# Band transfers of the attention head stage: described in four-byte words, and their reads issued by ScalarE

## The chip, the cores and the metric

The kernel runs on one core of a Trainium2 chip. The metric is device time in microseconds (us), the median of several runs. Beside the runs there is one profiled execution, from which all rows below come. Engines are named as in the profile: PE (TensorE matmul), PEld (its weight loads), DVE (VectorE), ACT (ScalarE), POOL (GpSimd), SP (SyncE, which issues transfers). SPq and POOLq are the sequencers of SP and POOL.

## What is computed

Four residual sublayers work on 2048 tokens of width 256: self-attention with 16 heads of width 16, a mixture of experts, a gated delta-rule attention, and a quantized feed-forward layer. Only the first one touches the change:

```python
q = (x @ q_w.T + q_b).reshape(B, S, H, Dh).transpose(0, 2, 1, 3)
k = (x @ k_w.T + k_b).reshape(B, S, H, Dh).transpose(0, 2, 1, 3)
v = (x @ v_w.T + v_b).reshape(B, S, H, Dh).transpose(0, 2, 1, 3)
q = apply_rope(q)
k = apply_rope(k)
attn = jnp.einsum('bhqd,bhkd->bhqk', q, k) * scaling
probs = jax.nn.softmax(attn, axis=-1)
```

## The kernel before

The program runs phase after phase. The first is `head_phase`, which makes Q, K and V; the second is `attention_phase`. A phase ends when every engine has done its instructions in it, and the next begins after that.

**What `head_phase` makes.** Q and K are kept as three bf16 parts each (high, middle, low), so that bf16 matmuls give float32 scores. For the score matmul each head needs a column of 96 rows, six bands of 16, in the tensors `q_t` and `k_t`. The projections come out with heads across the partitions, so the parts go through a scratch tensor in HBM, `qk_dram`, to change their layout: written by blocks, read back by bands.

**Blocks.** There are 16 blocks, n = 0 to 15. A block is one half of the heads (u), one of Q and K (side) and 512 tokens (b). Four blocks in a row (a group) share u and side; the groups come as Q, K, K, Q, for the halves 0, 0, 1, 1. Three buffers `parts` take the blocks in turn (`DEEP` = 3). The steps of one block are:

- PE projects it (L314); DVE adds the bias and applies the rotary tables (L389, twice); POOL adds the two products to `whole` (L277).
- `highest(n)` on ACT (L350) copies `whole` to bf16, the first part. It first waits until block n - 3 has been written out of the same buffer.
- DVE subtracts it (L396). `middle(n)` on ACT (L354) copies the rest to bf16. ACT's order is highest(n), middle(n - 1), highest(n + 1), and so on.
- `lowest(n)` on POOL (L282) makes the third part.
- `parts_away(n)` on SP (L235) writes the three parts to `qk_dram`, one transfer each: 128 partitions with a run of 512 bf16 (1 KB) each, 128 KB in all.

**Bands.** `heads_back(m)` on SP (L243) waits until the four blocks of group m have been written, and then reads the group back in three transfers, of 48, 32 and 16 rows. A row is 8 heads of 2048 tokens in bf16, 32 KB in one run, and goes to one partition. The three are 1536, 1024 and 512 KB, 3 MB a group. Below, R0 to R3 are the reads of groups 0 to 3, each of three transfers.

**Order on SP before.** All transfers of this stage are issued by SP, in program order: blocks 0 to 4, R0, blocks 5 to 8, R1, blocks 9 to 12, R2, blocks 13 to 15, R3.

**What waits for what.** `attention_phase` waits for R0 and R1 before its first matmul (heads of the first half), and for R2 and R3 only when it comes to the second half, in the middle of the phase. DVE's last work in `head_phase` are eight additions that take V out of PSUM (L414); they stand behind DVE's work on block 15 in its order.

Of the kernel before, what the change touches and what calls it, by code (L numbers as in the profile page):

```python
# [12 lines left out]
F32 = mybir.dt.float32  # L13
BF16 = mybir.dt.bfloat16
# [8 lines left out]
T = 2048  # L23
# [5 lines left out]
HEADS, DH = 16, 16  # L29
# [18 lines left out]
def flat(ap):  # L48
    names = "abcde"[: len(ap.shape) - 1]
    return ap.rearrange(f"p {' '.join(names)} -> p ({' '.join(names)})")  # L50
# [122 lines left out]
def head_phase(c, a, QT, KT, V, heads_in):  # L173

    nc = c.nc
    GROUPS, TILES = 4, NT // 4
    BT = TILES * P
    BLOCKS_QK = 4 * GROUPS
    HALF = HEADS // 2
    DEEP = 3  # L180
    PART_AT = ((0, 1, 2), (2, 1, 0))
    with ExitStack() as ctx:  # L182
# [11 lines left out]
        cosp, sinp, whole, rest = ([work[:, 2 * m + i, :] for i in range(2)] for m in range(4))  # L194
        parts = [f(f"parts{i}", [P, 3, BT], BF16) for i in range(DEEP)]
        tp = [c.ps(ctx, f"hd_tp{i}", [P, 2, KD, P]) for i in range(2)]
        plain = [c.ps(ctx, f"hd_plain{i}", [P, BT]) for i in range(2)]
        turned_ps = [c.ps(ctx, f"hd_rotated{i}", [P, BT]) for i in range(2)]
        v_ps = [c.ps(ctx, f"hd_v_ps{i}", [P, 2, D]) for i in range(2)]
# [3 lines left out]
        stats_done, var_done, rstd_done, scaled, _, turned, copied, _ = c.norm.values()  # L203
# [6 lines left out]
        parts_out = [c.sem(ctx, f"hd_parts_out{i}") for i in range(DEEP)]  # L210
        block = ctx.enter_context(nc.Block())

        def place(n):
            return n // (2 * GROUPS), (0, 1, 1, 0)[n // GROUPS], n % GROUPS

        @block.sync
        def _(sp):
            x = a["x"].rearrange("(t p) d -> p t d", p=P)
            for g in range(GROUPS):
                sp.dma_start(c.X[:, TILES * g:TILES * g + TILES, :], x[:, TILES * g:TILES * g + TILES, :]  # L220
                             ).then_inc(x_in[g], 16)
            sp.dma_start(W, a["wqkv"]).then_inc(s["w_in"], 16)
            sp.dma_start(bias[:, :], a["bqk"]).then_inc(s["tables_in"], 16)
            sp.dma_start(v_bias[:, :, :], a["bv"]).then_inc(s["tables_in"], 16)
            sp.dma_start(tables, a["rope"]).then_inc(s["tables_in"], 16)
            sp.wait_ge(s["one_set"], 1)
            sp.dma_start(KT[SPLIT_ROWS:SCORE_ROWS, 1:HEADS, :],
                         KT[SPLIT_ROWS:SCORE_ROWS, 0:1, :].broadcast_to([MAX_ROWS, HEADS - 1, T])
                         ).then_inc(s["ones_in"], 16)

            def parts_away(n):
                u, side, b = place(n)
                sp.wait_ge(s["lo_done"], n + 1)
                for part in range(3):
                    sp.dma_start(a["qk_dram"][side, u, part, :, :, BT * b:BT * b + BT].rearrange("d h t -> h d t"),  # L235
                                 parts[n % DEEP][:, part, :]).then_inc(parts_out[n % DEEP], 16)

            def heads_back(m):
                u, side, _ = place(GROUPS * m)
                for n in range(GROUPS * m, GROUPS * m + GROUPS):  # L240
                    sp.wait_ge(parts_out[n % DEEP], 48 * (n // DEEP + 1))
                for band, first, n in ((0, 0, 3), (3, side, 2), (5, 2 * side, 1)):
                    sp.dma_start(flat((QT, KT)[side][DH * band:DH * (band + n), HALF * u:HALF * u + HALF, :]),  # L243
                                 a["qk_dram"][side, u, first:first + n, :, :, :].rearrange("c d h t -> (c d) (h t)")
                                 ).then_inc(heads_in[u], 16)

            for n in range(BLOCKS_QK):
                parts_away(n)
                if n % GROUPS == 0 and n:
                    heads_back(n // GROUPS - 1)  # L250
            heads_back(BLOCKS_QK // GROUPS - 1)
            sp.wait_ge(s["ones_in"], 16)

        @block.gpsimd
        def _(pool):
# [17 lines left out]
            def put_together(n):  # L273
                pool.wait_ge(s["rot_read"], n + 1)
                if n >= 2:
                    pool.wait_ge(s["rest_done"], n - 1)
                pool.tensor_tensor(whole[n % 2], cosp[n % 2], sinp[n % 2], ALU.add  # L277
                                   ).then_inc(s["whole_done"], 1)
# [5 lines left out]

            for n in range(BLOCKS_QK + 1):
                if n < BLOCKS_QK:
                    put_together(n)
# [4 lines left out]
        def _(pe):  # L292
# [11 lines left out]
            def project(n):  # L304
                u, side, b = place(n)
                cols = 2 * P * (2 * u + side)
                if n < GROUPS:
                    pe.wait_ge(copied, was["copied"] + 2 * n + 2)
                for out, at, read, done in ((plain, cols, s["plain_read"], s["plain_done"]),
                                            (turned_ps, cols + P, s["rot_read"], s["rot_done"])):  # L310
                    if n >= 2:
                        pe.wait_ge(read, n - 1)
                    for k in range(KD):
                        last = pe.matmul(out[n % 2][:, :], W[:, k, at:at + P], c.XT[:, k, BT * b:BT * b + BT],  # L314
                                         start=(k == 0), stop=(k == KD - 1))
                    last.then_inc(done, 1)
# [11 lines left out]
            for g in range(GROUPS):  # L328
# [3 lines left out]
                else:  # L332
                    project(g - 1)
            for n in range(GROUPS - 1, BLOCKS_QK):
                project(n)
# [3 lines left out]
        @block.scalar  # L339
        def _(act):  # L340
            for i in range(NT // 2):
                act.wait_ge(turned, was["turned"] + i + 1)
                act.activation(c.XT[:, :, 2 * i * P:(2 * i + 2) * P].rearrange("p k (j c) -> p j k c", j=2),
                               tp[i % 2][:, :, :, :], ACT.Copy).then_inc(copied, 1)

            def highest(n):
                act.wait_ge(s["whole_done"], n + 1)
                if n >= DEEP:
                    act.wait_ge(parts_out[n % DEEP], 48 * (n // DEEP))
                act.activation(parts[n % DEEP][:, PART_AT[place(n)[1]][0], :], whole[n % 2], ACT.Copy).then_inc(s["hi_done"], 1)  # L350

            def middle(n):
                act.wait_ge(s["rest_done"], n + 1)
                act.activation(parts[n % DEEP][:, 1, :], rest[n % 2], ACT.Copy).then_inc(s["mid_done"], 1)  # L354

            for n in range(BLOCKS_QK + 1):
                if n < BLOCKS_QK:
                    highest(n)
                if n:
                    middle(n - 1)  # L360

        @block.vector
        def _(dve):
# [17 lines left out]
            def rotate(n):  # L381
# [4 lines left out]
                for out, ps, k, done, read in ((cosp, plain, 0, s["plain_done"], s["plain_read"]),  # L386
                                               (sinp, turned_ps, 1, s["rot_done"], s["rot_read"])):
                    dve.wait_ge(done, n + 1)
                    dve.scalar_tensor_tensor(out[n % 2], ps[n % 2][:, :], bias[:, at + k:at + k + 1],  # L389
                                             tables[:, k, BT * b:BT * b + BT], ALU.add, ALU.mult).then_inc(read, 1)  # L390

# [2105 lines left out]
def program(nc, a, out, only=None, upto=None):  # L2497
    with ExitStack() as ctx:
        c = Core(nc, ctx)
        if only in (None, "attn"):  # L2500
            with ExitStack() as attn:
                heads_in = [c.sem(attn, f"heads_in{i}") for i in range(2)]
                QT = c.sb(attn, "q_t", [P, HEADS, T], BF16)
                KT = c.sb(attn, "k_t", [P, HEADS, T], BF16)
                V = c.sb(attn, "v", [P, NT, HEADS, DH], F32)
                head_phase(c, a, QT, KT, V, heads_in)
                attention_phase(c, QT, KT, V, heads_in)
        if only in (None, "moe"):
            with ExitStack() as moe:
                rows = c.sb(moe, "moe_rows", [P, NT, D], F32)  # L2510
                inputs = MoeInputs(c, moe, a)
                attn_out_phase(c, a, rows, inputs)
                moe_phase(c, rows, a, inputs)
            if only == "moe":
                norm_phase(c, "ln2", True, want_t=False, out_dram=out)
                return
        elif only == "gdn":
            norm_phase(c, "ln2", False)
        if only in (None, "gdn"):
            delta_phase(c, a)  # L2520
            if only == "gdn":
                norm_phase(c, "ln3", True, want_t=False, out_dram=out)
                return
            tail_phase(c, a, out)
# [83 lines left out]
```

## Time and profile before

| | us |
|---|---|
| median of three runs | 3882.52 |
| lowest and highest of them | 3880.14, 3885.17 |
| the profiled execution's own time | 3883.3 |
| its span in the trace | 3881.6 |

The times of the rows are counted from the span's start. The head stage runs from 0 to about 145 us; the rest of the span belongs to the other phases.

### The profile page before, as it was taken

What the parts mean: (1) busy time and instruction counts of PE and PEld (TensorE: products, weight loads), DVE (VectorE), ACT (ScalarE), POOL (GpSimd) and SP (SyncE); (2) the same over time, 40 slices, a digit from 0 to 9 for tenths busy, and PEclk for the clock granted to TensorE, in tenths of its full rate; (3) what the DMA queues carried; (4) which work ended last, traced back from release to release, by engine and by line L of the source; (5) the groups of instructions that cost most, each with busy time, mean ns of one, the idle gap of its engine ahead of it and who ended that gap; (6) DMA issues with size and microseconds to landing.
All of it is one profiled execution on the core that took longest, in us unless ns stands there. A gap on an engine that the chain in (4) does not pass through costs nothing. (4 is left out here: it accounts for less than half of the span.)

```text
span 3881.6 us, 69297 instructions
## 1 busy us (share of the span) xinstructions
PE 3555.1 (92%) x22894; PEld 2220.9 (57%) x22894; DVE 2831.3 (73%) x6720; ACT 2428.1 (63%) x6502; POOL 1926.0 (50%) x4662
## 2 busy tenths in 40 slices
PE   6699999998896379999999999999999999999789
PEld 3133333333553247777777777777777777777645
DVE  4688888883423368888888888888888888888543
ACT  1066666666232367777777777777777777777411
POOL 3100000001302267877777777777777787777300
PEclk9599999999898589999999999999999999999999
DMA  6500000003222111111111110111111111111010
GB/s 162 95 1 1 1 1 1 1 1 128 96 81 86 34 27 30 39 33 30 40 34 28 41 41 21 40 41 29 32 41 31 38 33 41 30 36 25 16 37 17
DMA packets 201619, 149.25 MB, mean 38 GB/s; under 512 B 148740, under 2 KB 185732, under 8 KB 197681
## 3 DMA queue, kind: packets, MB, share of 16 engines
q1 hardware_dynamic: 198192, 136.42, 13.7%
q0 software_dynamic: 3072, 8.39, 0.7%
q8 instruction: 187, 3.06, 0.3%
q14 instruction: 168, 1.37, 0.1%
HBM read 102.69 MB, written 41.68 MB: 37 GB/s over the span
## 5 line engine op out<-in xcount | busy, mean ns | idle before, releaser
L2260 POOL TENSOR_TENSOR dl_blocks_tmp<-dl_blocks_l,dl_blocks_x 128x60 f32<-128x60 f32 (+24 forms) x1984 | 713.1, 359 | 307.4 <-DMA dl_blocks_l<-lm_dram 171.4
L2265 POOL TENSOR_TENSOR dl_blocks_x<-dl_blocks_x,dl_blocks_tmp 128x60 f32<-128x60 f32 (+24 forms) x1984 | 701.7, 354 | 155.4
L632 DVE TENSOR_REDUCE part_max<-mx 128x1 f32<-128x512 f32 x1024 | 637.0, 683 | 81.4 <-PE mx L494 81.3
L568 ACT ACTIVATE normed_t<-sc 128x1024 f32<-128x1024 f32 x512 | 496.4, 1021 | 222.1 <-PE sc L505 221.9
L2417 DVE SCALAR_TENSOR_TENSOR dl_conv<-dl_raw,dl_weights,dl_conv 128x512 f32<-128x512 f32 x768 | 580.7, 784 | 28.5 <-ACT dl_conv L2188 23.9
L1959 PE MATMUL prep<-normed_t,dl_weights 128*128 128x512 f32 x1024 | 484.2, 596 | 18.7 <-DMA dl_weights<-in_w_delta 17.3
L494 PE MATMUL mx<-k_t,q_t 96*128 96x512 bf16 x1024 | 375.0, 401 | 23.9 <-PEq L182 15.1
L475 POOL COPY v_staged<-v 128x256 f32<-128x256 f32 x16 | 6.3, 400 | 704.6 <-PE o_ps L517 704.6
L2118 ACT ACTIVATE dl_q_state<-rec_a,t_neg_decay 128x128 f32<-128x128 f32 x512 | 160.4, 366 | 239.4 <-DVE dl_r L2322 239.4
L505 PE MATMUL sc<-q_t,k_t 99*128 99x512 bf16 x1024 | 305.5, 381 | 0.6
L2128 ACT ACTIVATE dl_v<-rec_b,dl_s 128x128 f32<-128x128 f32 x512 | 164.9, 385 | 175.8 <-DVE dl_v L2330 97.2
L517 PE MATMUL o_ps<-normed_t,v_staged 128*32 128x512 f32 x2048 | 272.7, 605 | 0.4 <-ACT normed_t L568 0.4
L2064 PE MATMUL gate_y_ps<-dl_weights,dl_gated_t 128*128 128x256 f32 x1024 | 271.7, 388 | 0.9 <-ACT dl_gated_t L2133 0.9
L494 PEld LDWEIGHTS mx<-k_t,q_t 96*128 96x128 bf16 x1024 | 82.8, 97 | 324.3 <-DVE part_max L632 253.8
L2330 DVE TENSOR_TENSOR dl_v<-rec_b,dl_s_decayed 128x256 f32<-128x256 f32 x256 | 108.7, 425 | 213.6 <-PE rec_b L2037 204.7
L1959 PEld LDWEIGHTS prep<-normed_t,dl_weights 128*128 128x128 f32 x1024 | 176.7, 192 | 148.0 <-issue 144.3
L1973 PE MATMUL prep<-dl_weights,normed_t 128*128 128x256 f32 x1024 | 249.5, 387 | 0.0
L2289 POOL TENSOR_TENSOR dl_out_scale<-dl_out_scale,t_mhalf 128x2 f32<-128x2 f32 x256 | 185.9, 726 | 82.3 <-ACT dl_out_scale L2143 65.6
L2187 ACT ACTIVATE dl_raw<-prep 128x512 f32<-128x512 f32 x256 | 153.1, 598 | 102.4 <-PE prep L1959 102.3
L2322 DVE SCALAR_TENSOR_TENSOR dl_r<-rec_a,t_neg_decay,dl_v_scaled 128x128 f32<-128x128 f32 x512 | 155.2, 344 | 83.2 <-PE rec_a L2028 81.2
L2338 DVE SCALAR_TENSOR_TENSOR dl_state<-dl_state,t_chunk_decay,rec_a 128x128 f32<-128x128 f32 x512 | 153.8, 341 | 71.7 <-PE rec_a L2044 69.7
L1973 PEld LDWEIGHTS prep<-dl_weights,normed_t 128*128 128x128 f32 x1024 | 185.2, 191 | 22.6
(306 smaller groups left out, 7810.0 us busy)
## 6 DMA issues: line engine op xcount, KB each, us to landing
dl_blocks_l<-lm_dram SPq DMA_DIRECT2D x256, 128.0 KB, 2.7
dl_weights<-in_w_delta SPq DMA_DIRECT2D x16, 1032.0 KB, 4.9
lm_dram<-dl_lm SPq DMA_DIRECT2D x256, 32.0 KB, 1.7
xs_dram<-dl_blocks_x SPq DMA_DIRECT2D x64, 128.0 KB, 2.5
dl_inverse_t<-xs_dram SPq DMA_DIRECT2D x256, 32.0 KB
qk_dram<-hd_parts SPq DMA_DIRECT2D x48, 128.0 KB
rows_dram<-moe_zeros SPq DMA_DIRECT2D x1, 6016.0 KB, 23.1
moe_x_rows<-rows_dram SPq DMA_DIRECT2D x47, 128.0 KB, 2.2
```

What stands on the lines that cost most here:

```text
L494: pe.matmul(bank_of(x)[:, :], QT[0:SPLIT_ROWS, i, qt * P:(qt + 1) * P], KT[0:SPLIT_ROWS, i, b * 512:(b + 1) * 512], start=True, stop=True) ...
L505: last = pe.matmul(sc[u][:, b, :], KT[0:SCORE_ROWS, h, kt * P:(kt + 1) * P], QT[0:SCORE_ROWS, h, (2 * u + b) * BQ:(2 * u + b + 1) * BQ], s ...
L517: last = pe.matmul(o_ps[32 * qb:32 * qb + 32, :], vs[h % 2][:, kt, :], probs[:, kt % 2, qb * BQ:(qb + 1) * BQ], start=(kt == 0), stop=(kt ...
L568: act.activation(probs[:, e % 2, u * 2 * BQ:(u + 1) * 2 * BQ], flat(sc[u][:, :, :]), ACT.Exp, scale=float(DH) ** -0.5).then_inc(s["exp_don ...
L632: dve.reduce_max(part_max[:, t % NT, x[2]:x[2] + 1], bank_of(x)[:, :], AX.X).then_inc(s["ring_read"], 1)
L1959: last = pe.matmul(flat(bank[:, :, :]), proj_w(kh, k, m, 1), x_cols(k, q, 0, QT_), start=(k == 0), stop=(k == KD - 1))
L1973: last = pe.matmul(flat(PB[1 + u][:, 2 * j:2 * j + 2, :]), x_cols(k, q, (2 * u + j) * P, P), proj_w(kh, k, CH, VH), start=(k == 0), stop=( ...
L2064: last = pe.matmul(gy[:, 1, :], gt[g % 2][:, h, :], w_out(kh)[:, h, :], start=(h == 0), stop=(h == VH - 1))
L2260: pool.tensor_tensor(out, L[:, 0:i, i].unsqueeze(1).broadcast_to([P, NM - c0, i]), Xs[:, c0:NM, i:i + 1].broadcast_to([P, NM - c0, i]), AL ...
L2265: pool.tensor_tensor(Xs[:, c0:NM, 0:i], Xs[:, c0:NM, 0:i], out, ALU.add).then_inc(s["solve_step"], 1)
L2289: pool.tensor_tensor(osc[g % 2][:, :], osc[g % 2][:, :], tab["mhalf"], ALU.pow).then_inc(s["root_done"], 1)
L2417: dve.scalar_tensor_tensor(cv[:, m, :], raw[:, m, k:k + QT_], tap(kh, m, k), cv[:, m, :], ALU.mult, ALU.add).then_inc(s["conv_step"], 1)
```

## The change

The scratch tensor `qk_dram` is declared in float32 with half as many elements, and the on-chip ends of its transfers are viewed as float32. The bytes, their addresses and the length of each run stay as they were. `heads_back` moves from SP's program to ACT's: R0, R1 and R2 stand behind highest(n) and middle(n - 1) for n = 5, 9 and 13, R3 behind middle(15). SP issues the blocks alone, in order, without waits for earlier ones.

```diff
+    BW = BT // 2
...
-                    sp.dma_start(a["qk_dram"][side, u, part, :, :, BT * b:BT * b + BT].rearrange("d h t -> h d t"),
-                                 parts[n % DEEP][:, part, :]).then_inc(parts_out[n % DEEP], 16)
-
-            def heads_back(m):
-                u, side, _ = place(GROUPS * m)
-                for n in range(GROUPS * m, GROUPS * m + GROUPS):
-                    sp.wait_ge(parts_out[n % DEEP], 48 * (n // DEEP + 1))
-                for band, first, n in ((0, 0, 3), (3, side, 2), (5, 2 * side, 1)):
-                    sp.dma_start(flat((QT, KT)[side][DH * band:DH * (band + n), HALF * u:HALF * u + HALF, :]),
-                                 a["qk_dram"][side, u, first:first + n, :, :, :].rearrange("c d h t -> (c d) (h t)")
-                                 ).then_inc(heads_in[u], 16)
+                    sp.dma_start(a["qk_dram"][side, u, part, :, :, BW * b:BW * b + BW].rearrange("d h t -> h d t"),
+                                 parts[n % DEEP][:, part, :].bitcast(F32)).then_inc(parts_out[n % DEEP], 16)

             for n in range(BLOCKS_QK):
                 parts_away(n)
-                if n % GROUPS == 0 and n:
-                    heads_back(n // GROUPS - 1)
-            heads_back(BLOCKS_QK // GROUPS - 1)
...
+            def heads_back(m):
+                u, side, _ = place(GROUPS * m)
+                for n in range(GROUPS * m, GROUPS * m + GROUPS):
+                    act.wait_ge(parts_out[n % DEEP], 48 * (n // DEEP + 1))
+                for band, first, n in ((0, 0, 3), (3, side, 2), (5, 2 * side, 1)):
+                    act.dma_start(flat((QT, KT)[side][DH * band:DH * (band + n), HALF * u:HALF * u + HALF, :]).bitcast(F32),
+                                 a["qk_dram"][side, u, first:first + n, :, :, :].rearrange("c d h t -> (c d) (h t)")
+                                 ).then_inc(heads_in[u], 16)
...
             for n in range(BLOCKS_QK + 1):
                 if n < BLOCKS_QK:
                     highest(n)
                 if n:
                     middle(n - 1)
+                if n % GROUPS == 1 and n > GROUPS:
+                    heads_back(n // GROUPS - 1)
+            heads_back(BLOCKS_QK // GROUPS - 1)
...
-    aps["qk_dram"] = nc.dram_tensor("qk_dram", (2, 2, 3, DH, HEADS // 2, T), BF16).ap()
+    aps["qk_dram"] = nc.dram_tensor("qk_dram", (2, 2, 3, DH, HEADS // 2, T // 2), F32).ap()
```

## Rows read from the trace of the kernel before

**Rows 1.** Timeline of ACT: start us, length, line, operation, [idle before <-releaser].
```profile
42.03 0.61 ACT L354 ACTIVATE hd_parts<-q_t 128x512 bf16<-128x512 f32 x1
48.78 0.63 ACT L350 ACTIVATE hd_parts<-q_t 128x512 bf16<-128x512 f32 x1 [2.50 <-POOL q_t L277]
...
71.18 0.63 ACT L350 ACTIVATE hd_parts<-q_t 128x512 bf16<-128x512 f32 x1 [21.25 <-DMA qk_dram<-hd_parts]
...
74.82 0.63 ACT L350 ACTIVATE hd_parts<-q_t 128x512 bf16<-128x512 f32 x1 [2.49 <-POOL q_t L277]
...
104.77 0.63 ACT L350 ACTIVATE hd_parts<-q_t 128x512 bf16<-128x512 f32 x1 [21.53 <-DMA qk_dram<-hd_parts]
...
115.66 0.63 ACT L350 ACTIVATE hd_parts<-q_t 128x512 bf16<-128x512 f32 x1 [2.48 <-POOL q_t L277]
```

**Rows 2.** Timeline of SP: issues only, merged where one line issues several.
```profile
43.91 1.80 SPq L235 DMA_DIRECT2D qk_dram<-hd_parts  x3
45.89 1.28 SPq L243 DMA_DIRECT2D q_t<-qk_dram  x3
...
73.59 5.43 SPq L235 DMA_DIRECT2D qk_dram<-hd_parts  x6
79.19 1.28 SPq L243 DMA_DIRECT2D k_t<-qk_dram  x3
...
112.77 1.27 SPq L243 DMA_DIRECT2D k_t<-qk_dram  x3
...
143.22 1.23 SPq L243 DMA_DIRECT2D q_t<-qk_dram  x3
```

**Rows 3.** Windows: busy us of each engine, PE clock granted, DMA share, GB/s.
```profile
45.90:79.00 33.10, 18.09 (x38) 7.72 (x37) 8.13 (x12) 4.38 (x9) 9.53 (x8) 0.79 0.71 141
112.70:143.20 30.50, 12.57 (x48) 10.42 (x48) 6.73 (x10) 2.26 (x4) 4.64 (x4) 0.72 0.80 153
```

**Rows 4.** Transfers issued, 45.9 to 69 us: KB each, us to landing.
```profile
q_t<-qk_dram SPq DMA_DIRECT2D x1, 512.0 KB, 22.5
```

**Rows 5.** Timelines of DVE and POOL around the stage's end.
```profile
130.28 0.69 DVE L414 TENSOR_TENSOR v<-hd_v_ps,hd_v_bias 128x512 f32<-128x512 f32 x1 [1.03 <-PE hd_v_ps L323]
145.31 0.31 POOL L468 MEMSET v_staged<- 128x256 f32 x1 [26.15 <-POOLq L182]
```

**Rows 6.** DMA share in 40 slices: 41 to 45.8, 74.5 to 79, 136 to 143.2, 144 to 146.
```profile
DMA  0000434355555554555555541100000000344335
DMA  0004444455554554555545541000000000035443
DMA  4448444445565555555555555555444322100000
DMA  0009999900990900900000000000000000000000
```

**Rows 7.** DMA packets: windows 27.7 to 45.9 (1, 2) and 144 to 167 (3, 4).
```profile
DMA packets 1720, 1.69 MB, mean 93 GB/s; under 512 B 96, under 2 KB 1718, under 8 KB 1718
q1 hardware_dynamic: 1718, 1.66, 29.4%
...
DMA packets 147, 3.17 MB, mean 138 GB/s; under 512 B 48, under 2 KB 48, under 8 KB 48
q1 hardware_dynamic: 144, 3.15, 89.6%
```

**Rows 8.** DMA queues (packets, MB, share): 13 to 17, 144 to 146, 157.6 to 158.6 (two lines).
```profile
q1 hardware_dynamic: 103, 1.67, 98.0%
...
q1 hardware_dynamic: 16, 0.52, 163.0%
...
q1 hardware_dynamic: 11, 0.36, 175.5%
q14 instruction: 1, 0.01, 3.8%
```

**Rows 9.** DMA packets of POOL's queue, 1031 to 1060 us: its writes of rows.
```profile
DMA packets 1057, 2.90 MB, mean 100 GB/s; under 512 B 352, under 2 KB 352, under 8 KB 1056
```

## The prediction

> **What bounds the kernel now.** I looked first at what the change can touch. The chain that ended last lies in the last phase and says nothing of this one, so I read the head stage by its own rows: ACT's timeline, then SP's, then the transfers. ACT stands still twice for over 21 us, before highest(8) and before highest(12), each time for a block's write [rows 1]; nothing else on the path waits so long. SP's order says why. Block 5 is issued behind R0, block 9 behind R1, blocks 13 to 15 behind R2, and all of them share one queue [rows 2]. From R0's first issue (45.89) to highest(8) (71.18) are 25.3 us, from R1's (79.19) to highest(12) (104.77) 25.6 us; from the stall's end to the next read 8.0 us, both times. At the end SP waits for blocks 13 to 15 from R2's issue on, issues R3 at 143.22, and the next phase starts at 145.31 [rows 2, 5]. PE has about half of these stretches free, DMA engines are busy for 0.71 to 0.80 of them [rows 3]. So the stage is bound by three reads of about 25 us, each followed by what must happen before the next read can be issued.
>
> A read takes so long by itself: R0's third transfer landed 22.5 us after its issue [rows 4], which stands 0.86 us (two of three issues of 0.43) after the first [rows 2], so 23.4 us from the first issue. The rest, to 25.4, are the writes queued behind it.
>
> **Part 1, words of four bytes.** No byte or run is removed. The question is whether two-byte elements make the reads slow. From 144 to 167 us R3 runs alone: 144 packets, 48 of them small, so 96 rows of 32 KB, and 89.6% of 16 engines over 23 us is 3.43 us a row, or 9.5 KB/us [rows 7]. Float32 loads ran at 0.98 x 4 x 16 / 103 = 0.61 us for 16 KB, 26.9 KB/us [rows 8]. Upper bound of a gain: all of this ratio is due to the element, and the six rows that each engine has in a read (96 / 16) take 7.3 instead of 20.6 us, 13.3 us less, 40 us over R0 to R2. Lower bound: nothing; a loss is excluded, since runs and addresses stay. I take nothing, because the blocks' writes have the same two-byte elements and ran at 85.6 engine-us for about 1,620 rows of 1 KB, 53 ns each, 19 KB/us, twice the reads' rate [rows 7]; and because rows of one read, of one element, differ by transfer: 3.26 us for the first 16 rows, 2.55 us for those of 157.6 to 158.6 [rows 8].
>
> The Trainium skill, SBUF — State Buffer, Door 1, says that partitions 0 to 63 reach only 8 of the 16 ports by which transfers enter the buffer. By it the reads are slow because of their 48, 32 and 16 partitions, and words would give 0; by the first bound they would give 40 us. The rows that differ by transfer side with the page.
>
> **Part 2, the reads on ACT.** Removed from SP: four times three issues and their waits; SP never waits for a landing. Added to ACT: the same issues, 0.43 us each, and a wait for the group's blocks. Behind that wait stand highest(6), (10), (14) on ACT, for which DVE and POOL wait in turn; it makes ACT about 1 us late a group (free 42.64, below: R0 issued 44.9 to 46.2, the next highest due 3.6 after the one before). I cost it at nothing, because the stall that ends with the read comes right after and swallows it; without that cover it is some 3 us in all.
>
> The decisive part is what the write queue and the read queue, now two, do to each other on the DMA engines. What is late next:
>
> - R0. ACT has done middle(4) at 42.64 [rows 1], but must wait for block 3. Its data ran until 44.1 (slice 25 of 0.12 us), and a landing is signalled up to 0.9 us after the data: 142.3 for block 15, then R3 at 143.22 [rows 2, 6]. So R0 at 44.9, 1.0 earlier than before, its data 0.93 us later, at 45.8 (143.22 to 144.15 for R3 [rows 2, 6]).
> - Block 4, issued at 43.91, sends its data from 45.08 on [rows 2, 6], three transfers in some 2.6 us (as block 7, 74.84 to 77.4). The second and third meet R0. Before, block 4 was ahead of R0 and block 5 the first behind it. Now it is block 4 that is caught, and highest(7) waits for it.
> - How long. On each engine 16 rows of block 4 are left (8 of each transfer's 128) and six rows of R0. If the engine takes one packet of either queue in turn, and a packet is a row, six write rows go out between the reads and ten after them. A fetch of instructions got one turn in the middle of R3, while rows of R3 were still to start (157.6 to 158.6: 11 reads, 1 fetch) [rows 8], so a read does not hold an engine for its whole share; and SP's writes are recorded row by row, 1 KB a packet [rows 7]. So the write ends with the read. Bounds: 23.4 us after R0's issue (the read alone) and 25.4 (24 rows behind, as before); I take 24.5.
> - Then R1 needs block 7. Before, highest(8) began at 71.18 and block 7, issued at 73.59, had its data out at 77.4 and landed by about 78.2, 7.0 later [rows 1, 2, 6]. Now highest(7) comes first, and highest(8) 3.64 after it (71.18 to 74.82): 10.6 us from the stall's end to the next read instead of 8.0. Block 8 is caught by R1 in the same way: it is issued 3.6 after block 7, which lands 4.6 after its issue and so lets R1 go about 1 us behind block 8.
>
> Sum: R0 44.9; highest(7) 69.4; R1 80.0; highest(11) 104.5; R2 115.1; highest(15) 139.6. Before, highest(15) ran at 115.66, and DVE's last addition of V ended at 130.97, 15.3 later, under cover of R2 [rows 1, 5]. That cover is gone: now it ends at 154.9. Blocks 13 to 15 land before that, about 9 us after highest(15), so R3 is issued in time. With 0.86 us to the next phase (R3's last issue 144.45, then 145.31) it starts at 155.8, against 145.31: **10.5 us later**. With the bounds of the stall, three times, 7.2 to 13.2. The later phases are the same work and take no other time. The profiled execution, 3883.3, is 0.8 above the median of 3882.5; on the median the sum is 3893.0, on the bounds 3890 to 3896.
>
> **The rivals.** They turn on how many write rows pass between two read rows.
>
> - *Several rows a turn (no change).* POOL's queue shows that a packet can hold more than a row: 704 packets of 4 KB (1056 less 352 small ones) for rows of 1 KB [rows 9]. With four rows a turn block 4 needs four read rows of 3.43: highest(7) at 60.3, highest(8) with R0's end at 69, R1 at 76.0, then 31.1 us a read, R2 107.1, highest(15) 122.5, start 138.7: 6.6 less, 3876. Against it: SP's packets are rows.
> - *A whole share a turn on both sides (no change).* Block 4's two transfers wait for R0's first two (five rows): highest(7) 63.8, highest(8) 69, R1 76, R2 107, highest(15) 126, start 142.2: 3 less, 3879. Against it: the fetch in the middle of R3. The Trainium skill, DMA: Bandwidth & Descriptors, Queues, rings and completion order, has a rule beside it: an engine goes round its queues by packets, each typically of 9 to 17 descriptors. By it this rival would be the forecast.
> - *A transfer's share a turn for writes, a row for reads (faster).* Block 4 passes after two read rows, 53.5, block 5 after three more, 63.8; R1 70.8, R2 96.7; blocks 13 to 15 then end with R2 at about 122, start 124.5: 21 less, 3862.
> - *Writes pass freely (faster).* No stall: highest(8) 53.5, R1 60.5, R2 76, highest(15) 80.9, start 97.1: 48 less, 3835. This is the other side of my forecast by one mechanism; it decides from four rows a turn on, since with three the 16 rows of block 4 still need all six read rows. Nothing in the rows shows it, and the engines are 90% busy while a read is on [rows 7].
> - *Words work, one row a turn (faster).* 10.5 less 40: 3853.
>
> The Trainium skill, DMA: Bandwidth & Descriptors, Issuing engines are not separate DMA queues, says that starting transfers from several engines only saves issue time. SP's issue time ends no stall here, so by that rule the time would stay at about 3882.5; it lies within the chance of no change. The sum differs from it by the order in which reads and writes meet.
>
> **How the numbers follow.** The forecast 0.60; several rows a turn 0.09; whole shares on both sides 0.08; a share a turn for writes 0.09; free passing 0.06; words 0.06; a longer stall than the bounds 0.02. About 0.2% (8 us) is what a measurement of this kernel can tell from no change. Slower 0.62, same 0.17, faster 0.21. The likeliest case alone has 3890 to 3896. The range reaches down to the share a turn and leaves out free passing, words and a longer stall, with what lies above: 3860 to 3899.
>
> **What would show it.** Right: ACT's long idle times stand before highest(7), (11) and (15), of about 20 us each, put down to `qk_dram` writes; reads are issued near 45, 80 and 115 us; DVE's eight additions of V end the stage, near 155. The rows of the reads still take about 3.4 us. Wrong: rows of 1.2 us (words); stalls shorter than 10 us (writes pass); long stalls that still stand before highest(8) and (12) (block 4 slipped ahead of R0, as it may if its three transfers start 2 us earlier against the read).

## The result, and the profile of the changed kernel

| | before | after |
|---|---|---|
| median, us (20 runs each) | 3884.28 | 3893.25 |
| lowest and highest, us | 3880.14, 3890.03 | 3888.58, 3899.03 |
| ratio, 95% interval | | 1.0024 (1.0018 to 1.003) |
| profiled execution, us (span) | 3883.3 (3881.6) | 3890.92 (3889.2) |
| start of the next phase, from the span's start | 145.31 | 155.36 |

The change makes the kernel 0.24% slower. The forecast was slower, at 3893.0 us.

The first view to read is the timeline of the changed kernel: ACT with its issues, SP, the last addition of V on DVE, and POOL's first instruction of the next phase (beside [rows 1, 2, 5]; highest(n) is now L348).

```profile
45.30 1.78 ACTq L340 DMA_DIRECT2D q_t<-qk_dram  x3
...
69.62 0.63 ACT L348 ACTIVATE hd_parts<-q_t 128x512 bf16<-128x512 f32 x1 [21.29 <-DMA qk_dram<-hd_parts]
73.25 0.63 ACT L348 ACTIVATE hd_parts<-q_t 128x512 bf16<-128x512 f32 x1 [2.48 <-POOL q_t L266]
...
80.00 1.29 ACTq L340 DMA_DIRECT2D k_t<-qk_dram  x3
...
104.30 0.63 ACT L348 ACTIVATE hd_parts<-q_t 128x512 bf16<-128x512 f32 x1 [21.77 <-DMA qk_dram<-hd_parts]
...
114.66 1.44 ACTq L340 DMA_DIRECT2D k_t<-qk_dram  x3
...
139.40 0.63 ACT L348 ACTIVATE hd_parts<-q_t 128x512 bf16<-128x512 f32 x1 [22.05 <-DMA qk_dram<-hd_parts]
148.56 1.26 ACTq L340 DMA_DIRECT2D q_t<-qk_dram  x3
...
28.31 117.14 SPq L236 DMA_DIRECT2D qk_dram<-hd_parts  x48
...
154.38 0.69 DVE L415 TENSOR_TENSOR v<-hd_v_ps,hd_v_bias 128x512 f32<-128x512 f32 x1 [1.03 <-PE hd_v_ps L312]
...
155.36 0.31 POOL L469 MEMSET v_staged<- 128x256 f32 x1 [12.46 <-POOLq L183]
```

There are three long stalls where there were two, each of 21 to 22 us, each ended by the landing of a block's write, and each about 24 us behind the first issue of a read. They stand one block earlier than before, at highest(7) and highest(11), and the third, at highest(15), is new. The reads are issued at 45.30, 80.00 and 114.66. SP's 48 issues stand in one row, with no read between them. The stage now ends with V's last addition (155.07) and no longer with the issue of R3.

The table of waits says the same in one line: waiter, releaser, us in all, count, longest.

```profile
ACT hd_parts L348 <- DMA qk_dram<-hd_parts: 75.9, 6, 22.1
```

Three of the six are the stalls (21.29 + 21.77 + 22.05 = 65.1), the others 3.4 to 4 us before highest(6), (10) and (14). These stand behind the waits that ACT now makes for blocks 3, 7 and 11; the next stall swallows them.

The windows that answer to [rows 3] and the landing that answers to [rows 4]:

```profile
45.90:79.00 33.10, 16.77 (x33) 6.96 (x32) 7.49 (x12) 4.60 (x8) 8.02 (x7) 0.74 0.73 140
112.70:143.20 30.50, 5.39 (x21) 4.35 (x20) 4.13 (x7) 2.95 (x6) 7.02 (x6) 0.60 0.79 138
...
q_t<-qk_dram ACTq DMA_DIRECT2D x1, 512.0 KB, 22.8
```

A read takes what it took (22.8 us to the third landing, 22.5 before) at the same DMA share. In the second window PE's 12.57 us have become 5.39, and DVE's 6.73 have become 4.13: the last block and V stand behind the third stall.

How the two queues share the engines shows best while R0 runs: packets of 48 to 62 us, then by queue (packets, MB, share). q10 is ACT's, the reads; q1 is SP's, the writes.

```profile
DMA packets 126, 2.33 MB, mean 166 GB/s; under 512 B 20, under 2 KB 56, under 8 KB 56
q10 hardware_dynamic: 90, 2.29, 96.7%
q1 hardware_dynamic: 36, 0.04, 1.7%
```

Without the 20 small ones, which are all in the read's queue, there are 70 rows of the read (126 - 56) and 36 rows of writes (56 - 20): in 14 us the writes got 1.7% of the engines and one row for two of the read.

How much of block 4 was caught can be counted in the same way. Blocks 0 to 3 are out by 45 us, and block 5 is issued only near 50. The packets from 45 to 48 us:

```profile
DMA packets 271, 0.71 MB, mean 236 GB/s; under 512 B 15, under 2 KB 257, under 8 KB 257
```

So 242 of block 4's 384 rows (257 - 15) were out by then, and 142 were left, some 9 for each engine.

**Where 2.4 us came back.** The next phase starts 10.05 us later, but the span is only 7.6 longer. From the phase's start to the issue of `ao_w`, the first transfer that belongs to what follows (935.01 before, 943.67 after), it took 789.70 us before and 788.31 after, 1.4 less; the rest of the span, 2946.6 and 2945.5, 1.1 less. For the 1.4 the granted clock gives a hint: the window from 40 to 60 us behind the phase's start, first the kernel before, then the changed one (the number after the five engines is PE's clock).

```profile
185.30:205.30 20.00, 18.75 (x58) 4.98 (x59) 17.54 (x30) 6.31 (x7) 0.00 (x0) 0.63 0.01 1
```

```profile
195.36:215.36 20.00, 18.97 (x69) 5.11 (x69) 18.59 (x32) 7.51 (x9) 0.00 (x0) 0.70 0.01 1
```

The mean clock is 0.70 instead of 0.63 there (a mixture of 1.2 and 2.4 GHz), and PE does 69 matmuls instead of 58. Over the medians nothing of this can be made out: they differ by 8.97 us, and the stage, counted from block 0's first issue (27.75 before, 28.31 after), by 9.49.

### The profile page after: what moved, and what is told of

Same layout as the page of the kernel before. It is cut to its first block and busy times, and to the rows that moved or that the text cites. A ratio compares the mean times of both kernels' runs of the same rounds, so it can differ in the third digit from the quotient of the medians.

```text
span 3889.2 us, 69297 instructions
## 1 busy us (share of the span) xinstructions
PE 3555.9 (91%) x22894; PEld 2221.9 (57%) x22894; DVE 2830.7 (73%) x6720; ACT 2425.4 (62%) x6502; POOL 1929.8 (50%) x4662
## 5 line engine op out<-in xcount | busy, mean ns | idle before, releaser
L495 PE MATMUL mx<-k_t,q_t 96*128 96x512 bf16 x1024 | 372.8, 399 | 11.4 <-DVE part_max L633 10.4
## 6 DMA issues: line engine op xcount, KB each, us to landing
rows_dram<-moe_zeros SPq DMA_DIRECT2D x1, 6016.0 KB, 23.3
```

Source lines behind the costliest of these rows:

```text
L495: pe.matmul(bank_of(x)[:, :], QT[0:SPLIT_ROWS, i, qt * P:(qt + 1) * P], KT[0:SPLIT_ROWS, i, b * 512:(b + 1) * 512], start=True, stop=True) ...
```

## The experiments

All are read by two numbers: the time, against runs of the kernel before on the same chip, and the length of the stage in the trace, from block 0's first issue on SP to the next phase's first instruction. Before it is 145.31 - 27.75 = 117.56 us.

| run | stage, us | against before | median less that of before, us | ratio (95%) |
|---|---|---|---|---|
| after | 127.05 | +9.5 | +9.0 | 1.0024 (1.0018 to 1.003) |
| e1_words | 117.54 | 0.0 | -0.8 | 1.0002 (0.9993 to 1.0012) |
| e2_act | 127.50 | +9.9 | +8.6 | 1.0024 (1.0013 to 1.0035) |
| e3_block_ahead | 121.87 | +4.3 | +3.8 | 1.0012 (1.0002 to 1.0021) |
| e4_v_first | 122.57 | +5.0 | +3.6 | 1.001 (1.0 to 1.002) |
| e5_runs4k | 114.47 | -3.1 | -4.3 | 0.999 (0.998 to 0.9999) |
| e6_runs8k | 114.97 | -2.6 | -2.0 | 0.9993 (0.9983 to 1.0003) |
| e7_runs16k | 124.63 | +7.1 | +6.7 | 1.0017 (1.0008 to 1.0027) |
| e8_late | 103.84 | -13.7 | -12.0 | 0.9967 (0.9954 to 0.9979) |
| e9_late4k | 114.83 | -2.7 | -2.5 | 0.9995 (0.9986 to 1.0004) |
| e11_runs2k | 110.62 | -6.9 | -6.7 | 0.998 (0.9971 to 0.999) |
| e12_late4k_landed | 100.03 | -17.5 | -19.6 | 0.995 (0.9936 to 0.9963) |

The time follows the stage within some 2 us in every run, which is as well as this kernel's time can be measured.

**e1_words: the words alone.** The kernel before, with the float32 scratch and views; the reads stay on SP.

```diff
-    aps["qk_dram"] = nc.dram_tensor("qk_dram", (2, 2, 3, DH, HEADS // 2, T), BF16).ap()
+    aps["qk_dram"] = nc.dram_tensor("qk_dram", (2, 2, 3, DH, HEADS // 2, T // 2), F32).ap()
...
-                                 parts[n % DEEP][:, part, :]).then_inc(parts_out[n % DEEP], 16)
+                                 parts[n % DEEP][:, part, :].bitcast(F32)).then_inc(parts_out[n % DEEP], 16)
```

> Only the words of four bytes; the reads stay with SP, in the order of before. Forecast theory (words cost and bring nothing): the rows of the reads keep about 3.4 us, highest(8) stays near 71, highest(12) near 105, the next phase starts near 145.3, time within 3 us of before. Rival (words quicken the reads, and hide part of a larger loss by the other half of the change): rows below 3 us, time 10 to 40 us less. Rival (words are themselves the loss): 5 to 10 us more than before.

Queue of SP (packets, MB, share) from 145 to 168 us, while R3 runs alone:

```profile
q1 hardware_dynamic: 144, 3.15, 88.1%
```

That is 0.881 x 16 x 23 / 96 = 3.38 us a row of 32 KB; with two-byte elements 3.43 [rows 7]. The stage has its old length. The element does nothing here.

**e2_act: the reads on ACT alone.** The changed kernel with the scratch and the views in bf16.

```diff
-    aps["qk_dram"] = nc.dram_tensor("qk_dram", (2, 2, 3, DH, HEADS // 2, T // 2), F32).ap()
+    aps["qk_dram"] = nc.dram_tensor("qk_dram", (2, 2, 3, DH, HEADS // 2, T), BF16).ap()
```

> Only the reads on ACT; the elements stay bf16. Forecast theory: the whole loss is here, stalls before highest(7), (11), (15), next phase near 155.4, time 7 to 11 us above before. Rival (words are the loss): within 3 us of before.

Timeline of ACT:

```profile
71.33 0.63 ACT L348 ACTIVATE hd_parts<-q_t 128x512 bf16<-128x512 f32 x1 [21.57 <-DMA qk_dram<-hd_parts]
```

R0 was issued at 47.16, so highest(7) came 24.2 us behind it, as in the changed kernel. The whole loss lies in this half of the change.

**e3_block_ahead: the reads go one block later.** On ACT, each read also waits for the first block of the next group, so that this block is out before the read starts, as it was on SP.

```diff
-                for n in range(GROUPS * m, GROUPS * m + GROUPS):
+                for n in range(GROUPS * m, min(GROUPS * m + GROUPS + 1, BLOCKS_QK)):
```

> As after, but ACT issues a group's read only when the first block of the next group has landed too, so that this block is not caught. ACT waits longer than in after. Forecast theory (the loss is that one block more is caught by the read): R0 near 48.5, the stalls move back to highest(8) and (12), none before highest(15), R1 near 83.6, R2 near 119, the last blocks end with R2 and the next phase starts near 150, some 5 us earlier than after and 4 later than before. Rival (the loss is ACT's own waiting and issuing): more waiting on ACT, so the next phase starts at 158 or later.

Timeline of ACT:

```profile
48.49 1.30 ACTq L340 DMA_DIRECT2D q_t<-qk_dram  x3
...
73.49 0.63 ACT L348 ACTIVATE hd_parts<-q_t 128x512 bf16<-128x512 f32 x1 [18.81 <-DMA qk_dram<-hd_parts]
...
148.15 1.26 ACTq L340 DMA_DIRECT2D q_t<-qk_dram  x3
```

ACT issues and waits more than before, and still half of the loss is gone (+4.3 instead of +9.5). The stalls have moved back to highest(8) and highest(12), and there is no third: V's last addition ends at 140.34, and the stage ends with R3's issue, as before. So the loss isn't ACT's own waiting. What is left goes with the reads, which now wait for one block more: counted from block 0's issue, R0, R1 and R2 go 2.4, 4.5 and 6.0 us later than before (20.5, 55.9 and 91.0 instead of 18.1, 51.4 and 85.0).

**e4_v_first: V before the last remainder.** The changed kernel, with the eight additions of V moved ahead of DVE's subtraction for block 15.

```diff
+                if n == BLOCKS_QK:
+                    dve.wait_ge(s["rot_read"], BLOCKS_QK)
+                    for i in range(NT // 2):
+                        dve.wait_ge(s["v_done"], i + 1)
+                        dve.tensor_tensor(V[:, 2 * i:2 * i + 2, :, :].rearrange("p j h d -> p j (h d)"),
+                                          v_ps[i % 2][:, :, :], v_bias[:, :, :], ALU.add).then_inc(s["v_read"], 1)
                 if n:
                     remainder(n - 1)
...
```

> As after, but DVE takes V out of PSUM before its work on block 15's remainder, so within the stall. Forecast theory (the lost cover of V is the last term of the sum): highest(15) stays near 139.4, the stage then ends with R3's issue near 149.8, the next phase starts near 150.7, 4.7 us earlier than in after; up to 1.5 of it may be lost again as PE enters the next phase after an idle time. Rival (something else on the path after highest(15)): no change against after.

Timelines of DVE and ACT:

```profile
131.53 0.69 DVE L414 TENSOR_TENSOR v<-hd_v_ps,hd_v_bias 128x512 f32<-128x512 f32 x1 [1.03 <-PE hd_v_ps L312]
...
149.73 1.26 ACTq L340 DMA_DIRECT2D q_t<-qk_dram  x3
```

The three stalls are unchanged (highest(15) at 140.33), but V is done during the third, and the next phase starts at 151.41, right behind R3's issue. The stage is 4.5 us shorter than the changed kernel's: that is what the tail of V behind highest(15) costs beyond the next thing that is late, R3.

**e5, e6, e7 and e11: shorter runs.** If the writes are held up because they get their turn only between two long rows of a read, cutting the rows must let them through. The reads stay on ACT and move the same bytes. For e5 the scratch has 64 bytes of padding behind each head, so that a run ends there (4 KB); e11 has the same behind each half of a head (2 KB); e6 and e7 split each transfer into its even and odd runs of 8 and 16 KB. Of e5 and e6:

```diff
-    aps["qk_dram"] = nc.dram_tensor("qk_dram", (2, 2, 3, DH, HEADS // 2, T // 2), F32).ap()
+    aps["qk_dram"] = nc.dram_tensor("qk_dram", (2, 2, 3, DH, HEADS // 2, T // 2 + 16), F32).ap()
...
-                                 a["qk_dram"][side, u, first:first + n, :, :, :].rearrange("c d h t -> (c d) (h t)")
+                                 a["qk_dram"][side, u, first:first + n, :, :, 0:T // 2].rearrange("c d g t -> (c d) g t")
```

```diff
...
+                    here = a["qk_dram"][side, u, first:first + n, :, :, :].rearrange("c d (g i) t -> (c d) g (i t)", g=4)
+                    for odd in range(2):
+                        act.dma_start(there[:, odd::2, :], here[:, odd::2, :]).then_inc(heads_in[u], 16)
...
```

> As after, but the scratch tensor has 64 bytes of padding behind each head, so that a read is made of runs of 4 KB (48 for each engine) instead of rows of 32 KB (6). Bytes read and written are the same. Forecast theory (an engine takes one packet of either queue in turn): 16 write rows have passed after 16 runs, which is the time of two rows: highest(7) near 53.5 instead of 69.6, R1 near 71, R2 near 97, next phase near 124.5, about 20 us below before. Rival (a write waits for the whole read, however it is cut): stalls and time as in after.

> As after, but each read transfer is split in two that take the even and the odd runs of 8 KB (24 for each engine); three more issues on ACT a read, 1.3 us. Forecast theory: 16 write rows need 16 runs, the time of four rows: highest(7) near 60, R1 near 76, R2 near 107, next phase near 139, some 6 us below before. Rival (a write waits for the whole read): as after.

> As after, but each read transfer is split in two that take one run of 16 KB from each row (12 runs for each engine); three more issues on ACT a read, as with 8 KB. Forecast theory: 12 runs are fewer than the 16 write rows that are caught, so they still end with the read: highest(7) near 70, next phase near 155 to 158, time 8 to 12 us above before. Rival (more, shorter transfers help by themselves, whatever the count of runs): half of the way to the kernel with 8 KB.

> As the run with 4 KB, but padding behind each half head, so a read is made of runs of 2 KB (96 for each engine). With 4 KB highest(7) came 15.4 us after R0, not the 8.7 that one write row for each run gives. Theory 1 (while reads are on, a write row gets out about every 0.85 us at the most, however short the runs): again about 15.4 us, time as with 4 KB, some 4 us below before. Theory 2 (one write row for two short runs): 32 runs of 2 KB, highest(7) about 8.7 us after R0, time some 15 to 20 us below before. In both the read keeps its 24 us.

From a read's first issue to the end of the stall that follows, and the rows that passed in a stretch of R0 in which both queues had rows to send:

| runs | R0, R1, R2: us to the stall's end | forecast | stretch, us | write rows and read runs in it | read runs for one write row |
|---|---|---|---|---|---|
| 32 KB (after) | 24.3, 24.3, 24.7 | 24.5 | 48 to 62 | 36 and 70 | 1.9 |
| 16 KB (e7) | 23.2, 23.3, 24.3 | about 25 | 56 to 66 | 87 and 95 | 1.1 |
| 8 KB (e6) | 14.9, 17.4, 16.9 | about 15 | 59 to 64 | 59 and 127 | 2.2 |
| 4 KB (e5) | 15.4, 15.6, 15.4 | 8.7 | 59 to 66 | 150 and 298 | 2.0 |
| 2 KB (e11) | 14.1, 10.0, 10.6 | 15.4 or 8.7 (two theories) | 60 to 66 | 270 and 555 | 2.1 |

The lines from which the rows of e7, e6, e5 and e11 are counted (write rows are the packets under 2 KB without those under 512 B, read runs those of 2 KB and more). The last two are e5 from 45 to 56 us and e11 from 54 to 59:

```profile
DMA packets 254, 1.65 MB, mean 165 GB/s; under 512 B 72, under 2 KB 159, under 8 KB 159
...
DMA packets 220, 1.10 MB, mean 220 GB/s; under 512 B 34, under 2 KB 93, under 8 KB 93
...
DMA packets 475, 1.37 MB, mean 196 GB/s; under 512 B 27, under 2 KB 177, under 8 KB 475
...
DMA packets 857, 1.41 MB, mean 236 GB/s; under 512 B 32, under 2 KB 302, under 8 KB 857
...
DMA packets 721, 1.72 MB, mean 156 GB/s; under 512 B 21, under 2 KB 394, under 8 KB 721
...
DMA packets 356, 0.68 MB, mean 137 GB/s; under 512 B 13, under 2 KB 31, under 8 KB 356
```

The direction is as forecast: the shorter the runs, the sooner the write ends (at 16 KB hardly), and the loss turns into a gain at 8 KB and below (at 8 KB clear in the stage alone, since the interval of the time holds 1). The size isn't. The stages came out 2.6 us (e6), 3.1 (e5) and 6.9 (e11) below before; forecast were some 6, some 20, and some 4 or 15 to 20 by the two theories of e11. e7 lost 7.1, a little less than its 8 to 12.

Two numbers of the forecast differ from the rows. One write row passes not for one run of the read but for about two, at 32, 8, 4 and 2 KB alike, which is the turn of e11's second theory; at 16 KB it is one for 1.1. (The two kernels with six transfers instead of three also have bursts outside of these stretches: in e7 125 write rows pass beside 27 runs from 51 to 54 us.) And some 9 rows an engine were caught in the changed kernel, not 16. Nine rows at two runs each want 18 runs. That is more than the six of a read with 32 KB; by an estimate from these counts it is some 9 us of a read with 48 runs of 4 KB, and 4 us with 96 of 2 KB.

The stalls at 4 and 2 KB last longer than that. In e5 373 write rows (394 - 21) behind those of block 3 had passed by 56 us, and in e11 368 by 54, counted in the same way; block 4 has 384. Then few passed: in e11 18 (31 - 13) beside 325 runs from 54 to 59 us, although block 5 had been issued by then. What holds up the last dozen rows stays open.

Why so little of a stall that is 9 us shorter reaches the end is seen on ACT, in e5:

```profile
45.52 2.03 ACTq L340 DMA_DIRECT2D q_t<-qk_dram  x3
...
60.92 0.63 ACT L348 ACTIVATE hd_parts<-q_t 128x512 bf16<-128x512 f32 x1 [12.12 <-DMA qk_dram<-hd_parts]
70.62 0.63 ACT L348 ACTIVATE hd_parts<-q_t 128x512 bf16<-128x512 f32 x1 [8.55 <-DMA qk_dram<-hd_parts]
77.52 2.01 ACTq L340 DMA_DIRECT2D k_t<-qk_dram  x3
```

highest(7) comes 9 us sooner, but highest(8) then waits 8.55 us for block 5, which follows block 4 beside the same read and ends with it (R0's third transfer landed 23.0 us after its issue). R1 goes 2.5 us earlier than in the changed kernel, no more.

**e8_late: the second half's reads last.** The kernel before, with R2 and R3 behind all blocks on SP.

```diff
-                if n % GROUPS == 0 and n:
+                if n in (GROUPS, 2 * GROUPS):
                     heads_back(n // GROUPS - 1)
-            heads_back(BLOCKS_QK // GROUPS - 1)
+            for m in (2, 3):
+                heads_back(m)
```

> The kernel before, with R2 and R3 issued by SP after all blocks are written (elements bf16, reads on SP). Forecast theory (the stage's end is blocks 13 to 15 behind R2, which nobody needs yet): highest(15) stays near 115.7, blocks end near 124, V ends at 131, the next phase starts near 132, 13 us below before, some 1 us more if PE enters at full clock. Rival (the second half's reads then come too late or disturb the attention phase): part of it is lost there.

Timelines of SP and POOL:

```profile
123.60 1.28 SPq L243 DMA_DIRECT2D k_t<-qk_dram  x3
127.40 1.23 SPq L243 DMA_DIRECT2D q_t<-qk_dram  x3
...
133.15 0.31 POOL L469 MEMSET v_staged<- 128x256 f32 x1 [12.26 <-POOLq L182]
```

With R2 out of the way of blocks 13 to 15 the stage is 13.7 us shorter and ends with V. The time gains 12.0: the next phase, which now begins while both reads still run, takes 791.45 us instead of 789.70.

**e9_late4k and e12_late4k_landed: both edits together.** e9 has the 4 KB runs of e5 and issues R2 and R3 behind ACT's last middle(15). e12 adds a wait ahead of R2 for the last three blocks.

```diff
-                if n % GROUPS == 1 and n > GROUPS:
+                if n in (GROUPS + 1, 2 * GROUPS + 1):
                     heads_back(n // GROUPS - 1)
-            heads_back(BLOCKS_QK // GROUPS - 1)
+            for n in range(BLOCKS_QK - DEEP, BLOCKS_QK):
+                act.wait_ge(parts_out[n % DEEP], 48 * (n // DEEP + 1))
+            for m in (2, 3):
+                heads_back(m)
```

> Reads on ACT with runs of 4 KB, words of four bytes, and R2 and R3 issued after all blocks are written: the two gains together. From the run with 4 KB: R1 near 77.5, highest(11) near 93, highest(12) near 102; then no stall: highest(15) near 113, V ends near 128.5, the next phase starts near 130, some 15 us below before and 2 to 4 below the run that only issues R2 and R3 late. Rival (the late reads are what counts, and reads on ACT still add their wait): no better than that run.

> As the run with 4 KB and late reads, in which ACT issued R2 at 114.4, before blocks 13 to 15 were written, so that these were caught after all. Here ACT waits until all blocks have landed before R2. Forecast theory (blocks 13 to 15 were caught by R2 there): highest(15) stays near 113, blocks have landed near 121, R2 goes out then, V ends near 128, the next phase starts near 130 instead of 143.5, time 12 to 16 us below before. Rival (reads on ACT cost the end of the stage by themselves): the next phase still starts near 140.

Timeline of ACT in e9, then of ACT, DVE and POOL in e12:

```profile
114.37 1.89 ACTq L340 DMA_DIRECT2D k_t<-qk_dram  x3
140.90 1.88 ACTq L340 DMA_DIRECT2D q_t<-qk_dram  x3
```

```profile
122.00 1.89 ACTq L340 DMA_DIRECT2D k_t<-qk_dram  x3
124.07 2.89 ACTq L340 DMA_DIRECT2D q_t<-qk_dram  x3
...
127.04 0.69 DVE L418 TENSOR_TENSOR v<-hd_v_ps,hd_v_bias 128x512 f32<-128x512 f32 x1 [1.03 <-PE hd_v_ps L312]
...
128.01 0.31 POOL L472 MEMSET v_staged<- 128x256 f32 x1 [12.17 <-POOLq L183]
```

e9 missed, by the same mechanism. The end of ACT's program isn't the end of the writes: R2 waits for blocks 8 to 11 alone, so it was issued at 114.37, ahead of the last writes, and R3, which needs these, came 26.5 us later, when R2 was done. With the wait of e12 both are issued 2.1 us apart, and the stage ends with V. e12 takes 3864.58 us, 0.995 of the kernel before; it beats both kernels. Its median is 19.6 us below before, its stage 17.5, where 12 to 16 had been forecast.

## Why the prediction was right, step by step

| step | predicted | measured |
|---|---|---|
| R0 issued | 44.9 | 45.30 |
| highest(7) | 69.4 | 69.62 |
| R1 issued | 80.0 | 80.00 |
| highest(11) | 104.5 | 104.30 |
| R2 issued | 115.1 | 114.66 |
| highest(15) | 139.6 | 139.40 |
| V's last addition ends | 154.9 | 155.07 |
| next phase | 155.8 | 155.36 |

- *Words at nothing.* Right, measured alone by e1 (the same stage, 3.38 for 3.43 us a row); the rival of quicker words (3853 us) falls with it. The Trainium skill, SBUF — State Buffer, Door 1, has the bandwidth of a transfer depend on how many of the 16 ports its partitions reach. No run varied the partitions, so whether the ports make these rows slow stays open.
- *ACT's added waits at nothing.* Right: three of 3.4 to 4 us stand ahead of the stalls and are swallowed. e3, where ACT waits still longer and half of the loss goes, excludes them as the cause.
- *Block 4 is caught by R0 instead of block 5 following it.* Right, and the decisive part: the stalls stand at highest(7), (11) and (15), and they move back by one block when the read waits for that block (e3).
- *Length of a stall, 24.5, and 10.6 from there to the next read.* Measured 24.3, 24.3 and 24.7, and 10.4 twice.
- *One row of either queue in turn.* The effect is right: between rows of 32 KB the writes get so few turns that they end with the read. The sizes are not. The packets show one write row to two rows of the read, and about 9 rows of block 4 an engine were caught, not the 16 of the sum, because its second transfer was nearly out by 48 us, when R0 had sent 14 rows. The sum didn't suffer, since 9 rows too are more than the six of the read; the forecasts for shorter runs did. The rivals by which a read of these rows lets writes pass (3876, 3879, 3862, 3835 us) fall with the timeline of the changed kernel.
- *The lost cover of V.* Right: 15.67 us behind highest(15) instead of 15.3. Two errors cancel: the tail is 0.4 longer, and the next phase starts 0.29 us after it, not 0.86, which was the distance to R3's issue and not to V. e4 measures what this term costs: 4.5 us of the 9.5.
- *The later phases take no other time.* Off by -2.4 us in the profiled execution, 1.4 of them in the next phase beside a sooner rise of the clock; that the clock is their cause was not tested.
- *How near the number is.* That the median (3893.25) meets the forecast (3893.0) within 0.3 us is luck. The forecast difference was 10.5 us and the measured one is 9.0, and the median of the kernel before, 3882.52 with three runs, became 3884.28 with twenty. The times of the table also hold 0.56 us by which block 0 was issued later than in the profile before; counted from there, the stage grew by 9.5.

The Trainium skill, DMA: Bandwidth & Descriptors, Issuing engines are not separate DMA queues, says that issuing from several engines only saves the time of issuing; by that the time would have stayed at 3882.5. Here the ratio is 1.0024, and e2 puts all of it on the move from SP to ACT. That transfers of both engines interleave on the same DMA engines, as the section also says, is what the packets show; the price comes from who is caught behind whom.

Open: what sets one write row to two runs of the read, why 16 KB and some bursts let more pass, and what holds up the last dozen rows of a block beside short runs.

## What to carry to other kernels

When transfers move to another engine's queue, write down for each long one which short one is now caught beside it and which engine waits for that one; an order in one queue that looks like a needless wait may have kept a short write ahead of a long read. Here a bulk read that wasn't needed yet did best when it was issued behind the writes that the engines still waited for: behind them in the same queue (e8), or from another queue after a wait for their landing (e12), and not merely at the end of a program (e9). A stall that is removed in one place is worth only as much as the next wait allows, and a cover that was lost is priced by what it hid.

## What the runs showed of the hardware that was not expected

- Beside a read of three transfers on another queue, 1 KB writes got about one row for two runs of the read, whether the runs were 32, 4 or 2 KB long (36 to 70, 150 to 298, 270 to 555). Over the 16 engines that is 2.6, 21 and 45 write rows a microsecond.
- Beside runs of 2 KB (e11) 155 write rows passed from 48 to 54 us, the packets under 2 KB (169) less those under 512 B (14), and only 18 from 54 to 59.
- Runs of 4 KB cost a read next to nothing: its third transfer landed after 23.0 us, with rows of 32 KB after 22.8.
